# W2 as the stationary operand of the expert blocks: two experts on the two column halves, the sums copied out and turned back

## The reference, cut to what matters

```
gate_logits = xf @ Wg + bg
top_w, top_i = jax.lax.top_k(gate_logits, 2)
top_w = jax.nn.softmax(top_w, axis=-1)
for e in range(8):
    h = jax.nn.gelu(xf @ W1[e] + b1[e], approximate=False)     # 64 -> 256
    out = out + w_dense[:, e:e + 1] * (h @ W2[e] + b2[e])       # 256 -> 64
```

## Time and profile before

| | us |
|---|---|
| median of 3 runs | 472.03 (471.37 to 475.98) |
| the profiled execution, its own time | 471.31 |
| its span, first to last instruction | 469.5 |
| busy: PE / PE weight loads / DVE / ACT / POOL | 427.7 / 293.2 / 383.0 / 346.9 / 310.3 |
| mean granted clock of TensorE | 0.990 |

### The profile page before, as it was taken

The page is one execution under the profiler, slowest core; times in us unless marked ns, Lnnn a source line. Parts: engine busy times, 40 slices in busy tenths (PEclk is TensorE's granted clock), DMA queues, the critical chain, the costliest instruction groups (busy, mean ns, idle before and its releaser), DMA issues.

```text
span 469.5 us, 12098 instructions
## 1 busy us (share of the span) xinstructions
PE 427.7 (91%) x3633; PEld 293.2 (62%) x3633; DVE 383.0 (82%) x1321; ACT 346.9 (74%) x935; POOL 310.3 (66%) x450
## 2 busy tenths in 40 slices
PE   8898989899989889889889798878899999999995
PEld 8354444455635545445445444534799999999995
DVE  4598888777799898998998899998885788877632
ACT  2575587688788688688688675451888899999894
POOL 3243443756655787787787766854777777777775
PEclk9999999999999999999999989989999999999999
DMA  9918400000000000000000000102333222223320
GB/s 224 211 44 189 106 1 1 0 2 0 2 2 1 8 19 18 14 19 17 14 19 17 13 32 19 39 25 68 91 94 74 71 61 56 59 72 75 74 53 2
DMA packets 36168, 22.40 MB, mean 48 GB/s; under 512 B 13648, under 2 KB 33855, under 8 KB 36104
## 3 DMA queue, kind: packets, MB, share of 16 engines
q1 hardware_dynamic: 30264, 14.70, 14.3%
q0 software_dynamic: 4960, 6.45, 4.4%
q10 hardware_dynamic: 880, 0.48, 0.6%
HBM read 13.07 MB, written 9.27 MB: 48 GB/s over the span
## 4 chain that ended last, share of the span: by engine, by line
PE 50%; DVE 22%; POOL 13%; issue 11%; ACT 2%; DMA 1%; POOLq 0%; DVEq 0%; ACTq 0%
PE bank L1650 15%; PE bank L1587 5%; POOL pn L646 4%; PE dd L1636 4%; PE bank L1636 4%; DVE mx L1171 4%; POOL rows_hbm L621 3%; PE dd L1484 3%; PE bank L1503 3%; DVE sm L1179 3%; PE bank L1576 3%; PE bank L1553 2%; PE bank L1412 2%; DVE topi L963 2%; POOL out L666 1%
## 5 line engine op out<-in xcount | busy, mean ns | idle before, releaser
L646 POOL TENSOR_TENSOR pn<-pe_,rs 128x256 f32<-128x256 f32 x128 | 77.7, 629 | 88.7 <-DVE rs L1182 82.0
L621 POOL DMA_INDIRECT rows_hbm<-rowb,posu x64 | 65.6, 1026 | 23.7 <-issue 17.0
L666 POOL DMA_INDIRECT out<-bt,zs x63 | 63.1, 1001 | 20.0 <-issue 14.6
L1587 PE MATMUL bank<-pt,bt 128*128 128x256 f32 x256 | 66.7, 384 | 0.3 <-ACT zs L802 0.3
L789 ACT ACTIVATE pe_<-sc 128x512 f32<-128x512 f32 x64 | 40.6, 634 | 34.5 <-DVE sc L1174 30.4
L1171 DVE TENSOR_REDUCE mx<-dd 128x8 f32<-128x512 f32 x64 | 43.7, 683 | 13.9 <-PE dd L1484 13.8
L1484 PE MATMUL dd<-aa,bd 64*64 64x256 f32 x512 | 42.9, 406 | 9.5 <-DVE sc L1174 8.9
L1576 PE MATMUL bank<-ident,pn 128*128 128x128 f32 x256 | 40.1, 279 | 8.9 <-POOL pn L646 8.9
L1587 PEld LDWEIGHTS bank<-pt,bt 128*128 128x128 f32 x256 | 44.0, 192 | 3.9 <-issue 0.5
L797 ACT COPY pt<-bank 128x512 f32<-128x512 f32 x64 | 37.1, 580 | 12.6 <-PE bank L1576 12.3
L1174 DVE TENSOR_TENSOR sc<-dd,mx 128x512 f32<-128x512 f32 x64 | 44.3, 692 | 2.2
(11 more groups left out here) (316 smaller groups left out, 1097.8 us busy)
## 6 DMA issues: line engine op xcount, KB each, us to landing
zs<-rows_hbm SPq DMA_DIRECT2D x91, 66.0 KB, 1.9
wloc<-in_L_conv_w_local SPq DMA_DIRECT2D x2, 1152.0 KB, 9.1
rows_hbm<-zrow SPq DMA_DIRECT2D x1, 1914.0 KB, 14.0
x_sb<-in_x SPq DMA_DIRECT2D x3, 512.0 KB, 10.8
wloc<-in_L_ffn_W SPq DMA_DIRECT2D x2, 512.0 KB, 6.9
rows_hbm<-rowb,posu POOLq DMA_INDIRECT x64, 2.4
out<-bt,zs POOLq DMA_INDIRECT x63, 2.3
wrec<-in_w2b SPq DMA_DIRECT2D x1, 520.0 KB, 4.9
```

Of the source, the lines that this page charges most:

```text
L621: nc.gpsimd.indirect_dma_start(out=rows_hbm, out_offset=bass.IndirectOffsetOnAxis(ap=posu[:, t:t + 1], axis=0), in_=rowb[:, t], in_offset= ...
L646: ins = nc.gpsimd.tensor_tensor(pn[:, v % 2, :].rearrange("p (a y k c) -> p a k y c", a=PAIRS, k=2, c=WSZ)[:, :, k], pe_[:, v % 2, heads]. ...
L666: nc.gpsimd.indirect_dma_start(out=out, out_offset=bass.IndirectOffsetOnAxis(ap=idx_j, axis=0), in_=ob[:, j % LANES], in_offset=None, boun ...
L1587: last = nc.tensor.matmul(zo[:, :, :, w, :], bt[:, t % 2, 2 * v + w], pt[:, v % 2, :, w * WT:(w + 1) * WT], start=True, stop=True)
```

## The change

ffn2 exchanges the operands: W2 of an expert (128 x 64) is stationary and the hidden values (128 columns) move. Expert x writes partitions 64x to 64x + 63 of the bank, so that the two experts lie on the two halves of the array's columns; the products are ordered by hidden half first, then expert. The biases become two products with the biases stationary. The sums then stand turned: channels on the partitions, tokens along the row. VectorE copies them to SBUF (sums_out, 128 x 128 float32, double-buffered in yt, a view of an old tile), PE transposes them back (turned_back) into the next 128 columns of the same bank, and combine reads them there. On PE turned_back(j - 2) stands between rows_t(j + 2) and ffn2(j - 1); on VectorE sums_out(j + 1) stands ahead of combine(j). The loop on PE has one turn more.

```diff
+        yt = xn2[:].rearrange("p b t c -> p (b t c)")[:, 0:2 * P].rearrange("p (s n) -> p s n", s=2)
...
+            def sums_out(j):
+
+                wait(dve, ffn2_done, j + 1)
+                wait(dve, turned_done, j - 1)
+                nc.vector.tensor_copy(yt[:, j % 2], outb[j % 2][:, 0:P]).then_inc(yt_copied, 1)
+
             def combine(j):
...
-                wait(dve, ffn2_done, j + 1)
+                wait(dve, turned_done, j + 1)
                 wait(dve, stored[j % LANES], 16 * (j // LANES))
-                nc.vector.scalar_tensor_tensor(ob[:, j % LANES], outb[j % 2][:, 0:C], row[:, 2 * C:2 * C + 1], row[:, C:2 * C],
+                nc.vector.scalar_tensor_tensor(ob[:, j % LANES], outb[j % 2][:, P:P + C], row[:, 2 * C:2 * C + 1], row[:, C:2 * C],
...
+            sums_out(0)
             for j in range(BLOCKS):
+                if j + 1 < BLOCKS:
+                    sums_out(j + 1)
                 combine(j)
...
                 wait(pe, comb_ready, j - 1)
                 if j == TABLE + 2:
                     pe.wait_ge(table_ready, 2)
-                o = outb[j % 2][:, 0:2 * C]
-                nc.tensor.matmul(o, seq16[:, 1], weights_of(j)[:, :, R_B2:REC].bitcast(F16), start=True, stop=False, skip_group_check=True)
-                for q in range(4):
-                    x, k = q // 2, q % 2
-                    wait(pe, gelu_ready, 4 * j + q + 1)
-                    last = nc.tensor.matmul(o[:, x * C:(x + 1) * C], hh[:, j % 2, q], weights_of(j)[:, x, R_W2 + k * C:R_W2 + (k + 1) * C],
-                                            start=False, stop=(k == 1), skip_group_check=True)
+                o = outb[j % 2][:, 0:P]
+                for x in range(2):
+                    nc.tensor.matmul(o[x * C:(x + 1) * C, :], weights_of(j)[:, x, R_B2:REC].bitcast(F16), seq16[:, 1],
+                                     start=True, stop=False, skip_group_check=True)
+                for k in range(2):
+                    for x in range(2):
+                        wait(pe, gelu_ready, 4 * j + 2 * x + k + 1)
+                        last = nc.tensor.matmul(o[x * C:(x + 1) * C, :], weights_of(j)[:, x, R_W2 + k * C:R_W2 + (k + 1) * C], hh[:, j % 2, 2 * x + k],
+                                                start=False, stop=(k == 1), skip_group_check=True)
...
+            def turned_back(j):
+
+                wait(pe, yt_copied, j + 1)
+                nc.tensor.transpose(outb[j % 2][:, P:2 * P], yt[:, j % 2], ident[:]).then_inc(turned_done, 1)
+
...
-            for j in range(BLOCKS + 1):
+            for j in range(BLOCKS + 2):
                 if j < BLOCKS:
                     ffn1(j)
                 if j + 2 < BLOCKS:
                     rows_t(j + 2)
-                if j > 0:
+                if j > 1:
+                    turned_back(j - 2)
+                if 0 < j <= BLOCKS:
                     ffn2(j - 1)
```

More of the change, by code:

```diff
@@ L396, in program @@
         ffn2_done = sem("ffn2_done")
+        yt_copied = sem("yt_copied")
+        turned_done = sem("turned_done")
         comb_step = sem("comb_step")
@@ L1298, in _ @@
             last_blocks()
+            def sums_out(j):
+                wait(dve, ffn2_done, j + 1)
+                wait(dve, turned_done, j - 1)
+                nc.vector.tensor_copy(yt[:, j % 2], outb[j % 2][:, 0:P]).then_inc(yt_copied, 1)
             def combine(j):
                 row = xr[:, j % SLOTS]
-                wait(dve, ffn2_done, j + 1)
+                wait(dve, turned_done, j + 1)
                 wait(dve, stored[j % LANES], 16 * (j // LANES))
-                nc.vector.scalar_tensor_tensor(ob[:, j % LANES], outb[j % 2][:, 0:C], row[:, 2 * C:2 * C + 1], row[:, C:2 * C],
+                nc.vector.scalar_tensor_tensor(ob[:, j % LANES], outb[j % 2][:, P:P + C], row[:, 2 * C:2 * C + 1], row[:, C:2 * C],
                                                ALU.mult, ALU.add).then_inc(comb_step, 1)
                 dve.wait_ge(comb_step, j + 1)
-                nc.vector.scalar_tensor_tensor(ob[:, j % LANES], outb[j % 2][:, C:2 * C], row[:, 2 * C + 1:2 * C + 2], ob[:, j % LANES],
+                nc.vector.scalar_tensor_tensor(ob[:, j % LANES], outb[j % 2][:, P + C:2 * P], row[:, 2 * C + 1:2 * C + 2], ob[:, j % LANES],
                                                ALU.mult, ALU.add).then_inc(comb_ready, 1)
```

## The result

The changed kernel takes 496.02 us (median of 4 runs, 493.77 to 496.73) against 471.76 before (4 runs now, the 3 of the table and one more): ratio 1.0494, 95% interval 1.0443 to 1.0544. Its profiled execution took 493.8 us with a span of 492.0. Slower by 5%; the forecast was 495.

What follows compares the result with a forecast made beforehand. TensorE bounds the kernel before; after the change the ring does: 89 x 1.61 + 8.7 us of long turns = 152.0 against 128.9, +23.1, tail +0.4, on 471.3 gives 494.8, said as 495 us; range 484 to 503.

Steps and rivals of the forecast that it cites:

- The ring: Block stage: W2 of j-1, its copy, combine of j-2, then W2 of j form a closed loop, 1.61 us per block.
- The nearest copy row is longer: VectorE's copy of the sums: profile rows of similar PSUM copies exceed the Trainium skill's 0.26 us estimate; 0.29 was taken.
- The long turns: VectorE turns with register loads or table steps stall the block loop: 18 of 89, 8.7 us in all.
- TensorE's own block: TensorE's work per block in the changed kernel, waits aside: 1.45 us, the same as the period before.
- the two switches: TensorE changes tiling twice a block: 0.10 us each plus an uncovered load of 0.05, 0.30 in all.
- Nothing is won on TensorE: The 0.46 us per block saved by pairing W2 passes is paid back by two tiling switches and the transpose.
- the rival in which TensorE sets the pace: TensorE's 1.45 us per block bounds, long VectorE turns still stall: +13.1 us, so 485 us; chance 0.12.
- The Trainium skill's advice: Swap operands with 2x column tiling where the moving side is 64 wide or less: TensorE's block some 0.4 us shorter.
- The transpose's cover: TensorE's turning back is hidden: it needs the copy at 0.34 us and gets to it at 0.44.
- The tail: End of the kernel: 5.15 us from the last copy's start through POOL's last scatters, +0.4 us against before.

Runs made afterwards that it cites:

- opened by banks: The changed kernel with the turned-back sums in PSUM banks of their own, both experts' hidden values of a block sharing one bank: 478.55 us, ratio 1.0158.
- the same copy one block later: The kernel before with an unread copy of block j's sums on VectorE directly ahead of combine of block j: 472.87 us, ratio 1.0029.
- nearly a third of VectorE's load was taken away: The changed kernel without the weight copies of the full blocks, their register loads and waits: 488.33 us in one run.
- the kernel with the combine first: The changed kernel with combine of block j ahead of the copy of block j+1 on VectorE: 476.59 us, ratio 1.0089.
- the swap alone: The changed kernel without sums_out and turned_back, combine reading the turned sums where they lie: 468.14 us, ratio 0.9946.
- the copy ahead in the kernel before: The kernel before with an unread copy of block j+1's sums ahead of combine of block j on VectorE: 540.73 us in one run.

## Why the prediction was right

- **The ring.** Forecast 1.61, measured 1.59. Its terms: copy to combine 0.21 (0.21), combine 0.60 (0.59), VectorE to TensorE 0.05 (0.05), W2 from bias load to the copy 0.75 (0.74). The copy took 0.29 as taken from the median of the 512-element row; the estimate of 0.26 by the Trainium skill (VectorE: DVE Perf Modes, section on the TRN2 errata) was 0.03 short here. "The nearest copy row is longer" holds for that median (692 ns, 0.30 at 128 elements) but not for the shortest (641 ns, 0.25). That the ring is the cause is shown from four sides: opened by banks, opened by order, set up in the kernel before (and not set up there by the same copy one block later), and kept when nearly a third of VectorE's load was taken away.
- **The long turns.** Forecast 18 turns and 8.7 us, measured 18 and 8.6. Which turn is long had shifted by one block, as the steps stand behind a later copy.
- **TensorE's own block, mis-sized.** The step "TensorE's own block is then 0.50 + 0.16 + 0.30 + 0.055 + 0.43 = 1.45" gave too much: 1.34 once it ran freely. In the rows of the kernel with the combine first, the same terms are 0.51 (455.95 to 456.46), 0.11 for the transpose and 0.10 for the switch behind it (to 456.67), 0.08 for the bias (to 456.75), and 0.44 for the four pairs and 0.10 for the switch back (to 457.29). So the two switches cost 0.10 each, as read from the long passes, but no uncovered load of 0.05 came on top of either, and the transpose took 0.11, not 0.16. "Nothing is won on TensorE" was therefore wrong by 0.11 a block. It did not matter for the forecast, since the ring is longer than either (TensorE idles 1.59 - 1.34 = 0.25 a block, where I had 0.16), but the rival in which TensorE sets the pace would have given about 478, not 485. The Trainium skill's advice (TensorEngine Tiling, Performance Considerations) is borne out this far: the swap alone brought 1.45 to 1.23, transposes and copy included it is 1.34, if the waits allow it.
- **The transpose's cover.** "Hidden" was right, without the 0.10 of reserve: the transpose's load starts 0.34 after the copy, just when the copy is through.
- **The tail, mis-sized.** I had 5.15 us from the last copy to the end; it was 492.0 - 486.0 = 6.0. Rows of the end:

```profile
486.54 0.28 DVE L1317 SCALAR_TENSOR_TENSOR bt<-bank,zs,bt 128x64 f32<-128x64 f32 x1
...
487.62 0.97 POOL L669 DMA_INDIRECT out<-bt,zs  x1 [0.62 <-DVE bt L1317]
488.90 0.97 POOL L669 DMA_INDIRECT out<-bt,zs  x1 [0.30 <-issue]
```

  Block 89's combine ends at 486.82 and its scatter starts 0.80 later, where I had 0.06. In the kernel before, POOL's backlog hid this for most of the stage, but it was used up by block 84: the last blocks there have the same 0.80, so that it could have been read.
- **The total, partly luck.** The ring and its long turns came to 150.3 us for 152.0, -1.7, and the tail to +0.8. So the span is 492.0 for a forecast of 493.0. That the median of the runs, 496.0, lies within 1 us of the 495 is luck: the four runs spread over 493.8 to 496.7, and the two mis-sizes have opposite signs.

## What to carry to other kernels

When a step is inserted into an engine's order, list what is queued behind its wait, and follow who waits for that. If the path comes back to the producer of the inserted step, its length is a period of its own, however idle the engines are; here the ring was 1.59 on engines that needed 1.34. Put the consumer of the older block ahead of the step that waits for the newer one: moving one line was worth 19 us. And a faster producer is worth only what the last queue behind it (here POOL's scatters, one per 1.28 us from a fixed start) can take up.

## What the runs showed of the hardware

- Two 64-column tiles pair fully even in 128-column float32 passes: pairs 0.11 us apart, as fast as one pass with 128 columns loaded and 64 moved (0.111). The program gives one expert's product (two passes), then the other's, and the first passes of both still start 0.003 to 0.004 us apart, then the second ones.
- A change of tiling costs 0.10 us at these short passes too, as read from the long ones. In the kernel with the combine first, the last W2 pair starts 0.27 before the end of its record (456.75 + 0.60 - 0.27 = 457.08) and streams for 0.11; W1 follows at 457.29. The load behind the switch costs nothing more.
- An indirect transfer starts 0.80 us after the end of the combine that releases it, also where POOL had been idle for 1.99 us (block 72 of the changed kernel, at 460.52). In a backlog the next one starts 0.30 after the last.
- With the copy ahead in the kernel before, TensorE was busy 31.17 of 39 us with a wait of 0.40 in each turn, then waited 1.33 once; its granted clock fell from 1.00 to 0.50 and stayed there for the last 54 us, though TensorE, slower now, was busy 34.91 of 35 us. The changed kernel kept 1.00 through a turn as long. What brought the clock down, and why it did not rise, no run here separates.
